# Upper 36 rows of a 3x3 convolution: from F(2,3) in two groups to F(4,3) in one, with part of the low planes on GpSimd

## The reference

```python
residual = x
out = conv3x3_decomposed(x, lsq_quantize(w1, alpha1))
out = jax.nn.relu(batchnorm(out, gamma1, beta1))
out = conv3x3_decomposed(out, lsq_quantize(w2, alpha2))
out = batchnorm(out, gamma2, beta2)
out = jax.nn.relu(out + residual)
```

## Time and profile before

| | |
|---|---|
| time, median of 3 runs | 1667.34 us (1667.2 to 1667.58) |
| time of the profiled execution | 1667.43 us |
| its span, first to last instruction | 1665.6 us |
| TensorE (PE) busy | 1315.9 us, 79% |
| VectorE (DVE) busy | 1143.2 us, 69% |
| ScalarE (ACT) busy | 948.8 us, 57% |
| GpSimd (POOL) busy | 24.7 us, 1% |
| HBM read, written | 168.17 MB, 115.61 MB |
| mean granted TensorE clock | 0.904 |

### The profile page before, as it was taken

The page is one execution under the profiler, slowest core; times in us unless marked ns, Lnnn a source line. Parts: engine busy times, 40 slices in busy tenths (PEclk is TensorE's granted clock), DMA queues, the critical chain, the costliest instruction groups (busy, mean ns, idle before and its releaser), DMA issues.

```text
span 1665.6 us, 21380 instructions
## 1 busy us (share of the span) xinstructions
PE 1315.9 (79%) x6558; PEld 1176.1 (71%) x6558; DVE 1143.2 (69%) x1614; ACT 948.8 (57%) x1479; POOL 24.7 (1%) x30
## 2 busy tenths in 40 slices
PE   3999999999999999799999999999999940000000
PEld 2888888888888888688888888888888840000000
DVE  8877777777777777587777777777777765232332
ACT  2655555555555555577777777777777744222222
POOL 5000000000000000000000000000000000000000
PEclk9999999999999999899999999999999975555555
DMA  2444444444422221011112444442222189999998
GB/s 108 165 161 162 162 160 155 154 154 154 154 77 77 77 77 39 0 78 78 77 77 116 154 154 154 154 154 77 77 77 77 39 304 430 430 430 430 430 430 356
DMA packets 26661, 284.02 MB, mean 171 GB/s; under 512 B 3728, under 2 KB 3728, under 8 KB 4112
## 3 DMA queue, kind: packets, MB, share of 16 engines
q1 hardware_dynamic: 21456, 232.40, 35.5%
q10 hardware_dynamic: 5184, 51.38, 7.3%
HBM read 168.17 MB, written 115.61 MB: 170 GB/s over the span
## 4 chain that ended last, share of the span: by engine, by line
PE 78%; DMA 11%; another core or an unknown queue 5%; DVE 5%; issue 1%; ACT 0%; DVEq 0%; SPq 0%; POOL 0%; POOLq 0%; ACTq 0%
PE conv_psum L847 42%; PE conv_psum L865 36%; DMA xbuf<-in_x 8%; DMA slots<-conv_spill 3%; DVE slots L819 3%; DVE v_lo L656 1%; DMA slots<-in_L_conv_w 0%; DVE v_rows L653 0%; DVE v_rows L648 0%; DVE slots L279 0%; DVE slots L276 0%; ACT slots L604 0%; ACT v_hi L470 0%; ACT slots L523 0%
## 5 line engine op out<-in xcount | busy, mean ns | idle before, releaser
L656 DVE TENSOR_TENSOR v_lo<-v_rows,v_hi 128x1008 fp32r<-128x1008 f32 (+1 forms) x258 | 305.5, 1225 | 163.2 <-ACT v_hi L470 163.1
L847 PE MATMUL conv_psum<-v_hi,w2T 128*128 128x512 f32 x768 | 305.0, 397 | 8.7 <-DVE v_lo L656 8.5
L847 PE MATMUL conv_psum<-v_hi,w1T 128*128 128x512 f32 x768 | 305.6, 398 | 6.7 <-DVE v_lo L656 6.7
L847 PE MATMUL conv_psum<-v_lo,w1T 128*128 128x512 f32 x768 | 304.6, 397 | 0.0
L847 PE MATMUL conv_psum<-v_lo,w2T 128*128 128x512 f32 x768 | 304.1, 396 | 0.0
L470 ACT CAST v_hi<-v_rows 128x1008 fp32r<-128x1008 f32 (+1 forms) x258 | 260.4, 1034 | 61.0 <-DVE v_rows L648 47.5
L865 PE MATMUL conv_psum<-d_hi,w1T 128*128 128x398 f32 (+2 forms) x864 | 284.7, 333 | 0.0
L865 PE MATMUL conv_psum<-d_hi,w2T 128*128 128x398 f32 (+2 forms) x864 | 284.7, 333 | 0.0
L865 PE MATMUL conv_psum<-d_lo,w2T 128*128 128x398 f32 (+2 forms) x864 | 284.4, 334 | 0.0
L865 PE MATMUL conv_psum<-d_lo,w1T 128*128 128x398 f32 (+2 forms) x864 | 284.4, 334 | 0.0
L511 ACT ACTIVATE squares<-slots,minus_shift 128x1008 bf16 (+5 forms) x256 | 241.9, 945 | 14.4 <-ACT slots L498 13.1
(11 more groups left out here) (74 smaller groups left out, 1355.1 us busy)
## 6 DMA issues: line engine op xcount, KB each, us to landing
conv_spill<-slots SPq DMA_DIRECT2D x40, 1568.0 KB, 5.4
slots<-conv_spill SPq DMA_DIRECT2D x40, 1568.0 KB, 24.4
xbuf<-in_x SPq DMA_DIRECT2D x32, 1568.0 KB, 47.8
out<-slots ACTq DMA_DIRECT2D x32, 1568.0 KB, 11.8
slots<-in_x SPq DMA_DIRECT2D x31, 1568.0 KB, 7.4
slots<-in_L_conv_w SPq DMA_DIRECT2D x2, 576.0 KB, 8.1
slots<-in_x SPq DMA_DIRECT2D x1, 1036.0 KB, 9.1
slots<-in_x SPq DMA_DIRECT2D x1, 532.0 KB, 7.1
```

What stands on the lines that cost most here:

```text
L656: return nc.vector.tensor_tensor(v_planes(v_plane[t][1], first, end), v_made(first, end), v_planes(v_plane[t][0], first, end).bitcast(F32) ...
L847: last = nc.tensor.matmul(bank_run(GROUP_BANK[t] + k, PAIRS), w[:, M_WEIGHT[k] + kw, :], run(v_plane[t][half], k * PAIRS, (k + 1) * PAIRS, ...
```

## The change

The upper 36 rows go from F(2,3) to F(4,3): four output rows (instead of two) are made from six input rows by six products (instead of four). One group of nine tiles covers the 36 rows. The diff also changes who makes what and in which order.

- **Constants.** SLOTS 12 to 10 (so 22 images are spilled), XBUFS 5 to 6, 24 weight planes instead of 15. The weights of the six products are kept as integers by a common scale of 24, which alpha takes back (alpha / 24).
- **VectorE.** make_qp makes two intermediate row sets of image g + 1, q (2016 elements) and p (1008); make_v makes the six v sets from them. Only the low planes of the first of three pairs are made here. The products are combined by first_difference, second_difference, second_sum and rows_out; two results go back to PSUM. The taps of w2 are made integer and summed here, between steps 1 and 4.
- **GpSimd.** It makes the low planes of pairs 1 and 2 in each step; it has no part in the weights any more.
- **ScalarE.** Three high pairs per image, copies of m1 and m3, the last chunk of a step is evacuated in the next step, and the squares of an image are taken there too. The Relu runs two images ahead, in two parts. The transposed weights are copied in six pieces with a scale.
- **TensorE.** Six products of six matmuls, then the same three chunks, with chunks in banks 6, 7, 6. The second set of transposes comes after step 4, and step 5 waits for all its copies.
- **SyncE.** Loads are issued three images ahead. Of the six residual buffers one is loaded as soon as the second phase has begun, the others during and after the last step.

The core of the diff (lines that are only "..." mark what is left out; the functions removed are those named above):

```diff
-SLOTS = 12
-XBUFS = 5
+SCALE = 24.0
+SLOTS = 10
+XBUFS = 6
...
+    TILES = 9
+    WINO = 4 * TILES
+    N = TILES * W
+    CHUNKS = [(36, 43), (43, 50), (50, 56)]
+    NC = len(CHUNKS)
+    PITCH = W + 1
+    LEAD = 1
+    M = 6
+    PAIRS = M // 2
+    M_BANK = range(M)
+    CHUNK_BANK = [6, 7, 6]
+    D_ROWS = H - WINO + 1
+    D_PLANE = LEAD + D_ROWS * PITCH + 1
+    V_PLANE = LEAD + M * TILES * PITCH
+    RELU_PARTS = [(0, WINO + 1), (WINO + 1, H)]
+    NR = len(RELU_PARTS)
+    SUMS = TAPS + 12
+    WEIGHTS = TAPS + 15
+    M_WEIGHT = [12, 15, 18, 21, 9, 6]
...
+    COLS = SUM_COLS + NSQ
+    SPILL = IMAGES - SLOTS
+    STEPS = 2 * IMAGES
+    AHEAD = 3
...
+        def sum_taps(k, link):
+            g0, g1, g2 = (w_int[k][:, kh * 3 * C:(kh + 1) * 3 * C] for kh in range(3))
+            a, b, c, d = (w_int[k][:, (TAPS + 3 * j) * C:(TAPS + 3 * j + 3) * C] for j in range(4))
+            def stt(out, in0, scalar, in1):
+                return nc.vector.scalar_tensor_tensor(out=out, in0=in0, scalar=scalar, in1=in1,
+                                                      op0=ALU.mult, op1=ALU.add)
+            link(stt(b, g2, 1.0, g0))
+            link(stt(d, g2, 4.0, g0))
+            link(stt(a, g1, 1.0, b))
+            link(stt(b, g1, -1.0, b))
+            link(stt(c, g1, 2.0, d))
+            stt(d, g1, -2.0, d).then_inc(w_int_ready[k], 1)
...
 # SyncE
+            def phase1_load(m, b, old=None, lot=None):
+                sp.wait_ge(v_ready, (m - 2) * PAIRS + PAIRS)
+                if isinstance(m, int) and m == SLOTS - 2:
+                    sp.wait_ge(wT_ready, 2 * 6)
+                if isinstance(m, int) and m == SLOTS - 1:
+                    sp.wait_ge(w_int_ready[1], 1)
+                if old is not None:
+                    squared_through(old)
+                    sp.wait_ge(y1_stored[b], lot * 16 + 16)
+                sp.dma_start(slot(m), dram_image(xi, m)).then_inc(x_landed[b], 16)
...
+            sp.wait_ge(m_done, IMAGES * M + 1)
+            load_residual(0, 0)
+            sp.wait_ge(v_ready, STEPS * PAIRS)
+            load_residual(1, 1)
+            sp.wait_ge(lo_ready, last_step * LO + 1)
+            sp.wait_ge(pool_lo_ready, STEPS * PLO)
+            load_residual(2, 2)
+            sp.wait_ge(m_done, STEPS * M)
+            load_residual(3, 3)
+            load_residual(4, 4)
+            sp.wait_ge(chunk_done, STEPS * NC)
+            sp.wait_ge(rows_ready, STEPS * RR)
+            load_residual(5, 5)
...
 # GpSimd
+            def lo_of_pairs(g):
+                for k in (1, 2):
+                    pool.wait_ge(hi_ready, g * HI + (k + 1))
+                    nc.gpsimd.tensor_tensor(pair_window(1, k), pair_rows(k), pair_window(0, k).bitcast(F32),
+                                            ALU.subtract).then_inc(pool_lo_ready, 1)
+            pool.wait_ge(half_ready, 1)
+            for k in range(2):
+                with pool.Fori(k * IMAGES, (k + 1) * IMAGES) as g:
+                    lo_of_pairs(g)
+                pool.wait_ge(var_ready, k + 1)
+                nc.gpsimd.tensor_tensor(tiny[:, 1:2], tiny[:, 0:1], minus_half[:, :], ALU.pow).then_inc(powed, 1)
...
 # ScalarE
+            def take_weights(k):
+                def take(first, end, h, plane, scale):
+                    n = end - first
+                    nc.scalar.activation(wT[k][:, first:end, :],
+                                         w_bank(k, h)[:, plane * C:(plane + n) * C].rearrange("c (t o) -> c t o", o=C),
+                                         ACT.Copy, scale=scale).then_inc(wT_ready, 1)
+                act.wait_ge(transposed, 3 * k + 1)
+                take(0, 8, 0, 0, SCALE)
+                take(9, 12, 0, 0, SCALE / 4)
+                act.wait_ge(transposed, 3 * k + 2)
+                take(8, 9, 1, 0, SCALE)
+                take(12, 18, 1, 1, -SCALE / 6)
+                take(18, 19, 1, 7, SCALE / 24)
+                act.wait_ge(transposed, 3 * k + 3)
+                take(19, 24, 2, 0, SCALE / 24)
+            def hi_pairs(g):
+                for k in range(PAIRS):
+                    act.wait_ge(v_ready, g * PAIRS + (k + 1))
+                    if not (isinstance(g, int) and g == 0):
+                        act.wait_ge(m_done, g * M + (2 * k + 2 - M))
+                    nc.scalar.copy(pair_window(0, k), pair_rows(k)).then_inc(hi_ready, 1)
+            def take_m(g, j):
+                if not (isinstance(g, int) and g == 0):
+                    act.wait_ge(sums_ready, g * SR + (2 * j + 2 - SR))
+                act.wait_ge(m_done, g * M + (2 * j + 1))
+                nc.scalar.copy(rows_of((m1, m3)[j][:, :]), bank_rows(M_BANK[2 * j], TILES)).then_inc(m_copied, 1)
...
+            def step(g, p, b, phase, first=False, second=False, last=False, relu_next=None):
+                hi_direct(g, p)
+                if not first:
+                    take_chunk(g - 1, p + (SLOTS - 1), 1 - b, NC - 1)
+                take_m(g, 0)
+                if second:
+                    act.wait_ge(shift_ready, phase + 1)
+                if not first:
+                    square(g - 1, p + (SLOTS - 1), 1 - b, phase, 0)
+                take_m(g, 1)
+                if not first:
+                    square(g - 1, p + (SLOTS - 1), 1 - b, phase, 1)
+                    square(g - 1, p + (SLOTS - 1), 1 - b, phase, 2)
+                if not last:
+                    hi_pairs(g + 1)
+                if relu_next is not None:
+                    relu_next()
+                for j in range(NC - 1):
+                    take_chunk(g, p, b, j)
+            def finish_phase(g, p, b, phase):
+                take_chunk(g, p, b, NC - 1)
+                for part in range(NSQ):
+                    square(g, p, b, phase, part)
...
 # VectorE
+            def make_qp(g, p):
+                at_least(v_ready, g * PAIRS)
+                stt(q_rows[:, :], slot(p, -1, WINO - 1), -4.0, slot(p, 1, WINO + 1)).then_inc(qp_ready, 1)
+                nc.vector.tensor_tensor(p_rows[:, :].rearrange("c (i f) -> c i f", f=2 * W), two_of_four(p, 0, 2),
+                                        two_of_four(p, 0, 0), ALU.subtract).then_inc(qp_ready, 1)
+            def make_v(g):
+                v = [rows_of(v_rows[:, k * N:(k + 1) * N]) for k in range(M)]
+                dve.wait_ge(qp_ready, g * 2 + 1)
+                nc.vector.tensor_tensor(v[0], q_of(2), q_of(1), ALU.add)
+                nc.vector.tensor_tensor(v[1], q_of(2), q_of(1), ALU.subtract).then_inc(v_ready, 1)
+                dve.wait_ge(qp_ready, g * 2 + 2)
+                if not (isinstance(g, int) and g == 0):
+                    dve.wait_ge(pool_lo_ready, g * PLO - 1)
+                stt(v[2], p_of(0), 2.0, p_of(1))
+                stt(v[3], p_of(0), -2.0, p_of(1)).then_inc(v_ready, 1)
+                at_least(pool_lo_ready, g * PLO)
+                both = v_rows[:, 4 * N:6 * N].rearrange("c (two r w) -> c r two w", two=2, w=W)
+                q4 = q_rows[:, :].rearrange("c (i four w) -> c i four w", four=4, w=W)
+                nc.vector.tensor_tensor(both, q4[:, :, 2:4, :], q4[:, :, 0:2, :], ALU.subtract).then_inc(v_ready, 1)
+            def lo_of_pair(g, k):
+                dve.wait_ge(hi_ready, g * HI + (k + 1))
+                nc.vector.tensor_tensor(pair_window(1, k), pair_rows(k), pair_window(0, k).bitcast(F32),
+                                        ALU.subtract).then_inc(lo_ready, 1)
+            def lo_direct(g, p):
+                dve.wait_ge(hi_ready, g * HI + HI)
+                nc.vector.tensor_tensor(window(d_plane[1], 0, D_ROWS), rows_of(slot(p, WINO - 1)),
+                                        window(d_plane[0], 0, D_ROWS).bitcast(F32),
+                                        ALU.subtract).then_inc(lo_ready, 1)
+            m2, m3_bank, m4, m0, m5 = (bank_rows(M_BANK[k], TILES) for k in (1, 2, 3, 4, 5))
+            def first_difference(g):
+                at_least(rows_ready, g * RR)
+                dve.wait_ge(m_copied, g * 2 + 1)
+                dve.wait_ge(m_done, g * M + 2)
+                nc.vector.tensor_tensor(rows_of(d1[:, :]), rows_of(m1[:, :]), m2, ALU.subtract).then_inc(sums_ready, 1)
+                nc.vector.tensor_tensor(rows_of(s1[:, :]), rows_of(m1[:, :]), m2, ALU.add).then_inc(sums_ready, 1)
+            def second_difference(g):
+                dve.wait_ge(m_copied, g * 2 + 2)
+                dve.wait_ge(m_done, g * M + 4)
+                nc.vector.tensor_tensor(m3_bank, rows_of(m3[:, :]), m4, ALU.subtract).then_inc(sums_ready, 1)
+            def second_sum(g):
+                dve.wait_ge(sums_ready, g * SR + 3)
+                nc.vector.tensor_tensor(m4, rows_of(m3[:, :]), m4, ALU.add).then_inc(sums_ready, 1)
+            def rows_out(g, p, b):
+                d, s = rows_of(d1[:, :]), rows_of(s1[:, :])
+                d2, s2 = m3_bank, m4
+                def row(r, in0, scalar, in1):
```

(62 more changed lines are left out.)

506 lines of the change are left out of this document (180 added, 326 removed).

## The result

The changed kernel takes 1501.82 us (median of 4 runs, 1499.78 to 1503.96) against 1667.37 us for the kernel before: ratio 0.9007, 95% interval 0.8992 to 0.9023. The forecast was 1507, the range 1493 to 1550. The profiled execution took 1499.78 us around a span of 1497.7.

What follows compares the result with a forecast made beforehand. TensorE's matmul count was taken to bound the steps, then DMA transfers the tail: 26.6 + 64 x 17.63 + 2 x 2.6 + 5.0 + 20 = 1185.1, + 319.9 = 1505.0 of span, so 1507 us; range 1493 to 1550.

Steps and rivals of the forecast that it cites:

- First product: Start of TensorE's first product, after GpSimd's first pair and then VectorE's low pair: 26.6 us, before 28.89.
- End of the first step: First product at 26.6, plus one step of 17.63, plus 2.6 for slow first matmuls.
- Step: TensorE's step falls from 20.43 to 17.63 us, as 48 matmuls become 36; 64 steps give 179 us back.
- w2: TensorE waits for all six copies of w2's transposed weights: a hole of 5 us (4 to 8).
- Between the phases: TensorE's idle time between the two phases grows from 8.52 to 20 us, from squares, Relu, VectorE's work and GpSimd's lane.
- Second slow start: First 13 matmuls stand 0.44 apart instead of 0.233, costing 2.6 us, kept at both starts.
- Tail: From TensorE's end, transfers at 430 GB/s, 80 images instead of 79, +3.0 for squares: 313.2 becomes 319.9 us.
- The slack: make_qp, pushed by GpSimd, ends at 17.9; next lo_direct can't begin before 19.0: 1.1 us of room.
- GpSimd's price: Each 1008-element low pair on GpSimd taken as 2.5 us, between bounds of 2.4 and 3.6.
- The layout: Order within a step: VectorE's low pair from 8.2, rows_out until 13.7, GpSimd 9.4 to about 14.4; TensorE never waits.
- rival C: GpSimd also shuts out VectorE's operations with one PSUM input: step 20.9 us, total 1716 us; chance 0.11.
- Rival B: GpSimd's lane takes more than the slack: step 19.4 us, 113 us more, total 1620 us; chance 0.10.

Runs made afterwards that it cites:

- e1: Changed kernel with all three low pairs of an image made on VectorE, GpSimd idle: 1503.94 us.
- e8: Changed kernel plus one single-element tensor_tensor on GpSimd at the start, long before its first low pair: 1502.07 us.
- e11: Changed kernel in which VectorE, in the very first step, waits for GpSimd's first low pair before make_qp of the second image: 1497.48 us.
- e7: Changed kernel with squares of rows 0 to 35 before the last chunk's evacuation at phase ends, and step 5 awaiting w2's copies bank by bank: 1495.27 us.
- e9: e7 plus all low pairs of each phase's first image on VectorE, and that image's v0 and v1 made before p: 1492.15 us.
- e6: Changed kernel with XBUFS 5 instead of 6, one residual image fewer loaded before the tail: 1506.45 us.
- e10: e1 and e5 together: changed kernel with all low pairs on VectorE and low parts of products 3, 4, 5 left out: 1485.04 us.
- e2: Changed kernel in which GpSimd waits for the end of rows_out before its two low pairs, in all steps but the first: 1597.04 us.
- e4: Changed kernel in which GpSimd repeats its second low pair twice in every step: 1521.65 us.
- e5: Changed kernel without the low parts of products 3, 4 and 5, 9 of 90 matmuls a step, missing from the output: 1413.59 us.

## Why the prediction was right

Its terms against the profiled execution, in the order of its sum (predicted, measured; the measured ones are of one execution):

- **First product** 26.6, 24.06. **End of the first step** 26.6 + 17.63 + 2.6 = 46.8, 46.63. Right as a sum, by two errors that cancel. I let GpSimd take the lane before VectorE's low pair; VectorE had it first, so the first product came 2.5 earlier. But then VectorE kept it, and TensorE waited 2.23 for GpSimd's pair, of which the prediction knew nothing. That the sum came out within 0.2 is luck.
- **Step** 17.63, 17.57. The term that carries the sum: 2.86 us less a step than before, 183 in 64 steps. The price per matmul came from the earlier trace rows and held to 0.5%. 62 full steps at 0.06 less make 3.7 of the 7.3 us by which the span (1497.7) came out under the sum (1505.0).
- **w2** 5.0, 3.8: transposes from 116.90 (21 of 24 are in the trace), then ScalarE's copies until 120.66. The copies took 3.05 in place of 3.4, and the clock that I had allowed for was not lost in this execution: the granted clock was 1.00 over the next step (17.67 us). In the traces of e1, e8 and e11, which wait for the same copies as long, it was 0.91 and the step took 19.2.
- **Between the phases** 20, 18.30. Here VectorE got the lane before GpSimd, so the 2.2 for that was not paid. The squares cost 3.2 (from TensorE's end to the first sum of totals 4.6 us, before 1.4), and e7 gave 2.3 of that back. The terms that the prediction writes out for them make 2.8, not 3.0.
- **Second slow start** 2.6, 2.1 (613.53 to 633.22 is 19.69 for a step). In this trace 8 matmuls stand 0.43 apart or more before the distance falls to 0.23, in the earlier trace rows 13; in e9 it was 13 again, and that step took 20.45. The term is right only to about 1 us.
- **Tail** 319.9, 319.8. From TensorE's end to the first addition 8.2 us (1186.16), before 5.4: 2.8 for the squares. e6 supports the price of an image.

The step of the prediction on which all hung was VectorE's and GpSimd's. Its sum of VectorE's work was 15.9; e10 measures 17.46 with all low pairs, so 17.46 - 2 x 1.13 = 15.2 without two of them, and e2 gives the same (19.16 less two stretches of 2.0). The slack was 2.1 us, not 1.1. GpSimd's price, 2.5, was 2.2. The layout was right almost to the tenth: low pair 8.2 after the first product (410.22 - 401.83 = 8.4), rows_out until 13.7 (13.8), GpSimd 9.4 to 14.4 (9.4 to 13.8).

On the rule that carried this, the Trainium skill (SBUF — State Buffer, "Who interferes with whom") had two halves. The half that two SBUF inputs contend is borne out by e2 (3.19 and 3.33 us for 1.20 and 1.38). The half that one SBUF input does not contend is now shown as well: rows_out stays 0.60 apart under GpSimd. That excludes rival C. The same page of the Trainium skill ("Summary: rules for kernel authors") says that, where the two contend, the second one to issue blocks until the first one's instruction has finished. e2's lines agree; that GpSimd stayed out over six instructions at the start (8.87 us) goes beyond it.

Rival B named a real mechanism with a wrong price: with GpSimd's work doubled (e4), the kernel lost only 20 us in all, not 113, since the blocking first filled 2.1 us of idle time a step. Where both of GpSimd's operations meet operations with two SBUF inputs (e2) the cost is 95 us, near B's 113. Here the placement decided more than the amount.

What the prediction did not ask is what the move to GpSimd is worth. It priced it at nothing in cost and left its gain open; e1 shows a gain of 2 us of 1502, within the noise and none of it in the steady steps. The gain of the change is the count of products, nearly alone: 183 us in the steps, less what the edges and the tail took back.

## What to carry over

When one engine is full and without gaps, the price of a step is the count of its instructions by their start-to-start distance, and edges (first images, weight copies, the seam between phases) add up one by one; both can be read before the change is built. Moving work to a third engine pays only for what the engine relieved is late by. So lay out the whole step first, and put GpSimd's operations under those VectorE operations that take one of their two inputs from PSUM. Look at the order of starts too: when TensorE's step was shortened (e5), GpSimd came before VectorE's low pair in the second phase and stretched it. The chain of a first step deserves its own layout, since waits that a steady step hides lie bare there.

## What the hardware showed that was not expected

- VectorE can keep GpSimd waiting over a whole row of operations with two SBUF inputs: 8.87 us for an operation of 2.14, from 22.82 to 31.7. With a wait put into VectorE's row it took 3.12 (e11). In e2 and e4 the two alternated instead. The cause of the difference is open.
- The executions of the changed kernel differ more than those of the kernel before: 1499.78 to 1503.96 (0.28%) against 1667.2 to 1667.58 (0.02%). All variants of it show 1 to 4 us of spread. The record shows a part of the reason: the mean granted clock of these four executions falls from 0.888 in the shortest to 0.885 in the two longest. Between traces the difference lies in the steps after TensorE's holes. After w2's copies, a hole of 2.41 us in each, the step takes 17.67 us at granted clock 1.00 in the changed kernel and in e6, but 19.2 at 0.91 in e1, e8 and e11, where some 8 matmuls stand 0.43 us apart, the distance of the 1.2 GHz level. What decides between the two is not shown. It is also why differences of 1 to 3 us between medians should be read from the traces.
